# Neighbourhood attention: softmax sums by products with ones, division at the read-out

## The reference, cut to what matters

```python
attn = jnp.einsum('bhijc,bhikjlc->bhijkl', q, k_win)
attn = attn + bias.transpose(0, 1, 3, 2, 4)[None]
attn = jax.nn.softmax(attn.reshape(B, nh, H, W, K * K), axis=-1)
attn = attn.reshape(B, nh, H, W, K, K)
out = jnp.einsum('bhijkl,bhikjld->bhijd', attn, v_win)
```

## Time and profile before

| | |
|---|---|
| median of 3 executions | 7745.3 us (7731.54 to 7747.34) |
| profiled execution | 7755.66 us |
| its span, first to last instruction | 7753.8 us |
| busy share of the span: PE, DVE, ACT, POOL | 92%, 69%, 52%, 48% |
| mean granted clock of TensorE | 0.938 of full speed |
| `layer0_attend`, by its first and last scores | 287.5 to 1128.2 us of the span |
| largest groups of the stage, busy us: L682 ACT, L582 PE, L689 ACT, L579 PE, L629 DVE, L639 DVE | 468.1, 423.1, 391.9, 373.9, 349.1, 332.5 |

### The profile page before, as it was taken

One profiled execution on the slowest core, in us unless ns is written; L12 is line 12 of the kernel. 1 busy time (PEld: TensorE's weight loads), 2 busy tenths in 40 slices (PEclk: granted clock), 3 DMA queues, 4 the chain that ended last, 5 costly groups with the idle time before them and its releaser, 6 DMA issues. The chain is left out here.

```text
span 7753.8 us, 151401 instructions
## 1 busy us (share of the span) xinstructions
PE 7122.0 (92%) x47408; PEld 4321.3 (56%) x47408; DVE 5352.3 (69%) x12827; ACT 4036.6 (52%) x9389; POOL 3715.9 (48%) x2394
## 2 busy tenths in 40 slices
PE   8699989989999999999999999999999888619998
PEld 5477766645455455455555554554554334518888
DVE  5598886689677677677677676776776004518888
ACT  2498982200465665566555555655566663114443
POOL 5111112100466666566566566665666675355553
PEclk9899999955899999999999999999999999759999
DMA  8534327730111201201202102102112003512211
GB/s 243 122 70 93 71 75 244 242 85 0 32 26 38 60 23 45 54 25 44 53 24 52 46 25 58 39 24 68 30 27 58 3 5 115 162 36 58 62 57 31
DMA packets 404353, 508.79 MB, mean 66 GB/s; under 512 B 65616, under 2 KB 358402, under 8 KB 399751
## 3 DMA queue, kind: packets, MB, share of 16 engines
q1 hardware_dynamic: 380887, 457.79, 22.7%
q0 software_dynamic: 22640, 40.75, 1.8%
HBM read 316.59 MB, written 188.86 MB: 65 GB/s over the span
## 5 line engine op out<-in xcount | busy, mean ns | idle before, releaser
L1380 DVE TENSOR_REDUCE a_tops<-a_ps 128x1 f32<-128x448 f32 (+1 forms) x5600 | 3073.7, 614 | 1092.5 <-PE a_ps L1282 1075.4
L1503 POOL TENSOR_TENSOR a_added<-a_P 128x896 f32<-128x896 f32 x1344 | 2801.7, 2105 | 2094.6 <-ACT a_P L1480 2094.6
L1480 ACT ACTIVATE a_P<-a_ps 128x448 f32<-128x448 f32 (+1 forms) x5600 | 2657.1, 547 | 2123.9 <-PE a_ps L1351 2088.4
L1351 PE MATMUL a_ps<-a_qp,a_kp 98*128 98x448 f32 (+1 forms) x5600 | 2158.6, 401 | 100.9 <-ACT a_P L1480 69.8
L1282 PE MATMUL a_ps<-a_hk,a_hq 96*128 96x448 f32 (+1 forms) x4900 | 1818.0, 381 | 1.2 <-DMA a_hq<-scratch_q 1.1
L1351 PEld LDWEIGHTS a_ps<-a_qp,a_kp 98*128 98x128 f32 (+1 forms) x5600 | 1031.8, 188 | 1296.1 <-ACT a_P L1480 735.1
L1302 PE MATMUL a_ps<-a_P,a_vt 128*32 128x448 f32 (+1 forms) x11200 | 1337.0, 549 | 0.0
L1282 PEld LDWEIGHTS a_ps<-a_hk,a_hq 96*128 96x128 f32 (+1 forms) x4900 | 916.8, 187 | 262.5 <-DVE a_tops L1380 170.6
L1318 PE MATMUL a_ps<-a_added,a_ones 128*32 128x448 f32 x5376 | 649.0, 555 | 0.0
L1302 PEld LDWEIGHTS a_ps<-a_P,a_vt 128*32 128x32 f32 (+1 forms) x11200 | 290.1, 109 | 514.0 <-issue 384.1
L1403 DVE RECIPROCAL a_sums<-a_sums 128x112 f32<-128x112 f32 x224 | 185.3, 836 | 488.8 <-ACT a_sums L1455 488.8
(11 more groups left out here) (196 smaller groups left out, 7783.8 us busy)
## 6 DMA issues: line engine op xcount, KB each, us to landing
a_qp<-scratch_q SPq DMA_DIRECT2D x168, 224.0 KB, 3.8
a_kp<-scratch_k SPq DMA_DIRECT2D x96, 320.0 KB, 5.0
a_hk<-scratch_k SPq DMA_DIRECT2D x84, 336.0 KB, 5.2
scratch_t<-o_ts SPq DMA_DIRECT2D x56, 448.0 KB, 5.7
n_vt<-scratch_vw SPq DMA_DIRECT2D x64, 343.0 KB
a_hq<-scratch_q SPq DMA_DIRECT2D x84, 200.0 KB, 3.2
e_w<-in_w SPq DMA_DIRECT2D x16, 1024.0 KB
a_hq<-scratch_q SPq DMA_DIRECT2D x84, 192.0 KB, 3.4
```

The source lines that it names most:

```text
L1351: pe.matmul(PS[0:rows_of(t), i_s % 3, 0:GW], kp[0:98, hh, 128 * t:128 * t + rows_of(t)], qp[0:98, hh, GW * j:GW * j + GW], start=True, sto ...
L1380: dve.tensor_reduce(tops[0:rows_of(t), KT * hh + t, k:k + 1], PS[0:rows_of(t), bank, 0:GW], AX_X, ALU.max).then_inc(topped, 1)
L1480: act.activation(P[0:rows_of(t), (2 * n + pair) % (2 * RING), hh % 2, :], PS[0:rows_of(t), (4 * n + hh) % 3, 0:GW], ACT.Exp).then_inc(expe ...
L1503: pool.tensor_tensor(added2[:, a % 6, :, :], P[:, (2 * n + pair) % (2 * RING), :, :], P[:, (2 * n + 2 + pair) % (2 * RING), :, :], ALU.add ...
```

## The change

The sums of P no longer come from ScalarE, and P is no longer divided ahead of its transposes. The transposes work on the undivided exponentials, and `mix` is followed by 24 more instructions of the same shape, in which a matrix of ones (32 columns) takes the place of V: their result, in columns 128 to 239 of the same PSUM bank, is the sum of P for each head and position, repeated over the head's 32 output channels. `read_out` takes the reciprocal of these 128 x 112 sums and multiplies the output with it. `normalise` is gone, with its semaphore, and so are the unit products of `turn`, which now waits for the exponential itself. The ones of the third chunk's first 14 rows are zero, since those keys stand in the second chunk as well.

```diff
-        rs = sb("rs", [TT, 8])
-        rc = sb("rc", [TT, 8])
+        ones = sb("ones", [CHUNK, 2, 32])
+        rc = sb("rc", [128, 2, TT])
...
                     since(pe, copied, it, U, bank_free_at(m) + 1)
-                    pe.matmul(PS[0:TT, turn_bank(m), 384:384 + TT], idn[:, :], idn[:, :], start=True, stop=True)
-                    pe.wait_ge(normed, it * U + m + 1)
+                    pe.wait_ge(exped, it * U + m + 1)
...
                 for c in range(3):
                     for hh in range(4):
                         last = pe.matmul(PS[32 * hh:32 * hh + 32, OUT, 0:TT], vt[:, rb % 2, tc, c, 32 * hh:32 * hh + 32],
+                                         PTs[:, (4 * n + hh) % 8, TT * c:TT * c + TT], start=(c == 0), stop=(c == 2))
+                for c in range(3):
+                    for hh in range(4):
+                        last = pe.matmul(PS[32 * hh:32 * hh + 32, OUT, 128:128 + TT], ones[:, c // 2, :],
                                          PTs[:, (4 * n + hh) % 8, TT * c:TT * c + TT], start=(c == 0), stop=(c == 2))
                 last.then_inc(mixed, 1)
...
-            def normalise(it, n, pair):
-                m = 4 * n + 2 * pair
-                dve.wait_ge(exped, it * U + m + 2)
-                dve.reciprocal(rc[:, m % 8:m % 8 + 2], rs[:, m % 8:m % 8 + 2]).then_inc(inverted, 1)
-                dve.wait_ge(inverted, it * (U // 2) + m // 2 + 1)
-                for k in (m, m + 1):
-                    dve.tensor_scalar(P[:, k % RP, :], P[:, k % RP, :], rc[:, k % 8:k % 8 + 1], None, ALU.mult)\
-                       .then_inc(normed, 1)
...
                 dve.wait_ge(mixed, it * NBLK + n + 1)
+                dve.reciprocal(rc[:, n % 2, :], PS[:, OUT, 128:128 + TT]).then_inc(inverted, 1)
                 if tc == 0:
                     since(dve, stored, it, 4 * 16, 16 * (rb - 3))
-                dve.tensor_copy(yT[:, 14 * W * rb:14 * W * (rb + 1)].rearrange("p (i c) -> p i c", c=W)[:, :, 8 * tc:8 * tc + 8],
-                                PS[:, OUT, 0:TT].rearrange("p (i s) -> p i s", s=SUB)).then_inc(out_read, 1)
+                dve.wait_ge(inverted, it * NBLK + n + 1)
+                dve.tensor_tensor(yT[:, 14 * W * rb:14 * W * (rb + 1)].rearrange("p (i c) -> p i c", c=W)[:, :, 8 * tc:8 * tc + 8],
+                                  PS[:, OUT, 0:TT].rearrange("p (i s) -> p i s", s=SUB),
+                                  rc[:, n % 2, :].rearrange("p (i s) -> p i s", s=SUB), ALU.mult).then_inc(out_read, 1)
...
-                act.activation(P[:, m % RP, :], sm[:, m % 4, :], ACT.Exp, bias=mx[:, m % 8:m % 8 + 1], scale=-1.0,
-                               accum_out=rs[:, m % 8:m % 8 + 1]).then_inc(exped, 1)
+                act.activation(P[:, m % RP, :], sm[:, m % 4, :], ACT.Exp, bias=mx[:, m % 8:m % 8 + 1], scale=-1.0)\
+                   .then_inc(exped, 1)
```

More of the change, by code:

```diff
@@ L456, in layer0_attend @@
         scored, maxed, exped, inverted = sem("scored"), sem("maxed"), sem("exped"), sem("inverted")
-        normed, turned, copied = sem("normed"), sem("turned"), sem("copied")
+        turned, copied = sem("turned"), sem("copied")
         mixed, out_read, stored = sem("mixed"), sem("out_read"), sem("stored")
@@ L610, in _ @@
             pe.wait_ge(consts, 16)
+            pe.wait_ge(padded, 3)
             pe.wait_ge(zeroed, 2)
@@ L658, in body @@
                     maxima(it, n)
[L659 to L666, removed]
             dve.memset(qn[:, :, :], 0.0).then_inc(zeroed, 1)
             dve.memset(vt[0:14, :, :, 2, :], 0.0).then_inc(padded, 1)
+            dve.memset(ones[:, :, :], 1.0).then_inc(padded, 1)
+            dve.wait_ge(padded, 2)
+            dve.memset(ones[0:14, 1, :], 0.0).then_inc(padded, 1)
             for it in range(ITS):
                 body(it, it == 0, it % B == 0)
-            for pair in range(2):
-                normalise(ITS - 1, NBLK - 1, pair)
             for n in range(NBLK - 4, NBLK):
```

## The result

The changed kernel takes 8182.5 us (8181.59 to 8184.39) against 7745.6: 437 us more, a ratio of 1.0568 with a 95% interval of 1.0551 to 1.0585. The prediction said 8230, in a range of 7890 to 8290.

A forecast was written before the change was run, and what follows sets the result against it. A ring of waits between VectorE, ScalarE and TensorE bounds one stage: 223 turns of 5.86 us make 1307, with 20, 1 and 5 added 1333, 491 more than 842; so 8230 us, range 7890 to 8290.

The forecast's parts named there:

- What bounds the stage: In the one changed stage: waits between VectorE, ScalarE and TensorE bound each block, 763 of 841.7 us.
- the ring: Chain of waits from a block's first maximum to the next block's: 3.42 us before, 5.86 forecast after.
- ScalarE: Exponential to copy: without reading the accumulator, 0.09 us leaves the step, 0.53 becoming 0.44; ScalarE's own bound 3.1 us.
- Products with ones: TensorE, between the product with V and the next scores: 24 more instructions, 0.57 us at full clock, 1.14 at 1.2 GHz.
- Read-out: VectorE, scores' start to next maximum: 1.21 us in place of 0.54, with 0.86 for the reciprocal.
- The clock: TensorE's granted clock: falls to 1.2 GHz and stays low over the stage, raising the ring from 4.38 to 5.86 us; chance 0.62.
- a hole of some 1.4 us in each block: TensorE idle between three heads' turns and the copy's end, at a ring of 4.38 us; the clock was expected to fall.
- the rival of a clock that stays up: TensorE stays at full clock: ring 4.38 us, 169 us more, 7915 us in all; chance 0.15.
- From the freed bank to V at the lower clock: TensorE's fourth turn, from the PSUM bank being freed to `mix`, at 1.2 GHz: 0.82 us.
- The longer stretches: Blocks running beyond the steady ring: 78 us before the change, 0 to 78 may remain, 20 kept.
- the stalled divisions: VectorE divisions beside GpSimd's copy, two taking 2.62 us in place of 0.64: stalls should go, gain at most 32 us.
- The sum: Whole stage: 1333 us in place of 842, so 491 us more.

The follow-up runs named there:

- e5: Changed kernel reordered, same instructions: TensorE issues next scores ahead of V and ones, VectorE does maxima ahead of read-out; 7682.5 us, 0.9930 of the kernel before.
- e4: Changed kernel without the products with ones, reciprocal and multiplication reading the output itself; 7930.4 us, 1.0245 of the kernel before.
- e1: Changed kernel with the unread unit products put back ahead of the transposes; 7956.5 us, 1.028 of the kernel before.
- e7: Changed kernel with unread unit products for only the first three heads of each block; 7888.3 us, 1.0185 of the kernel before.
- e2: Kernel before without its unread unit products, all else as before; 7754.3 us against 7732.9, ratio 1.0026.
- e3: Changed kernel with a reciprocal of 2 columns in place of 112, a constant for the others; 7754.5 us, 1.0018 of the kernel before.

## Why the prediction was right, point by point

- **What bounds the stage.** Right. The same waits in the same order make the ring after the earlier trace rows; e5, which cuts it without removing an instruction, gives some 490 us back.
- **ScalarE.** Right: exponential to copy 0.44, as worked out. The gain of 0.09 is real but lies in a ring that other terms lengthen.
- **Products with ones.** Right: 1.14 forecast at the lower clock, 1.12 measured (the block is that much shorter in e4). V and ones together take 2.40 (904.98 to 907.38) for 2.42.
- **Read-out.** Right: 0.86 taken for the reciprocal, 0.858 measured; its wait 0.03 (902.66 - 901.77 - 0.86), the multiplication to the maximum 0.19 for 0.18. The row of a reciprocal out of SBUF was the right neighbour; the upper bound with a whole PSUM copy was not needed.
- **The clock.** Right in its level, 0.50 for the whole stage, and partly by luck. I put it at 0.62. The step rested on a likeness, not on a cause, and its mechanism, a hole of some 1.4 us in each block behind which the clock falls, is not what happened. The clock was at 0.50 before the first block and did not rise, and at that clock the turn waits only 0.20 us for its copy. e1 and e7 show that unit products bring the clock up, e2 that without them it swings, and e3 that a shorter ring holds it without them. In e7 the turn waits 0.59 and the clock is up: idle time alone does not decide, and neither does an unbroken run. What it is in the unit products that does is open. The Trainium skill ("TensorE: Matmul & The Clock Gate", section "HAM oscillation — how this bites in real kernels") puts falls down to longer idle gaps and so led to the rival of a clock that stays up. e7 agrees with it; the fall behind 1.10 us does not; and the changed kernel, whose clock never came up in the stage, is no test of it.
- **From the freed bank to V at the lower clock.** A little too dear: 0.82 forecast, 0.73 measured. I had taken the first step of a unit product for that of a transpose. With 0.02 in other steps the ring is 5.75 for 5.86, which is 25 us.
- **The longer stretches.** Oversized: 20 us kept, where 1277.3 is even below 223 x 5.75 + 1 = 1283. With the ring at 4.33 and the clock up (e7) 14 us of them are left: what held the blocks up before has gone with the divisions or is hidden in the longer ring, and no run tells the two apart. The bound of 32 us on the stalled divisions was too low: by the mean of 414 ns for a division on the page before, against a median of 365, the 896 divisions had about 896 x 0.049 = 44 us of it. This does not move the sum, in which the stalls were one part of the 78. The stalls of the division beside GpSimd's copies are gone as said: no maximum lasts over 0.451 us, no reciprocal over 0.859, no multiplication over 0.277. The Trainium skill ("SBUF — State Buffer", section "Who interferes with whom") has it so for operations with at most one SBUF input, and these rows agree.
- **The sum.** 491 us forecast for the stage, 436 measured; the two items above are 51 of the 55.

## What to carry to other kernels

Before adding an instruction to an engine that has time to spare, follow the waits of one block round to where they close: 0.86 us on VectorE, which the same change had relieved of its divisions, was worth some 415 us, because it stood in the ring. When a good idea makes a kernel slower, try its instructions in another order before dropping it: scores ahead of the products, maxima ahead of the read-out turned 5.7% slower into 0.7% faster. And before removing work that nobody reads from TensorE, look at the granted clock of the stage with and without it.

## What the runs showed of the hardware

The granted clock stayed at 0.50 for the 1270 us of a window in which TensorE was busy for 96% of the time by the records, and at 1.00 in e1, where it was busy for 639 of 740 us (86%). A busy TensorE is no sign that its clock is up; at the lower clock the same work simply takes longer to be busy with. Nor did 10.60 us without a hole raise it, at the start of the changed kernel's stage.

A kernel can run at two paces that go with the clock: in e2 blocks of 4.23 us and blocks of 3.40 us follow each other in stretches, with the same instructions.

The reciprocal of 128 x 112 numbers takes 0.858 us out of PSUM beside 0.842 out of SBUF, three times the copy of the same tile; the source made 0.016 us.
